# Edge tiles of 128 rows in two gather stages, and the edge network moved from the first of them into the second

## The chip, the cores and the metric

The kernel runs on one core of a Trainium2 chip. The metric is the device time of one execution in microseconds, the lower the better. The five engines of the core each run their own instruction stream in order: PE (TensorE, matrix products), DVE (VectorE), ACT (ScalarE), POOL (GpSimd) and SP (SyncE, which here only issues transfers). They meet through semaphores. Transfers run on the core's 16 DMA engines.

## The reference, cut to what matters

Two layers of a graph network on 6250 nodes (N) of 256 features (D) with 100000 edges (E), sorted by their destination. In both layers each node gets a sum over its incoming edges, of rows of the source nodes. In the second layer each row is weighted first, by four numbers of the edge; these are its attribute (4 values, `edge_attr_4`) times one number that a small network makes of the edge's 10 other values:

```
x -> layer norm -> xn
layer 0: agg[dst] += xn[src] for all edges;  MLP with batch norm of agg
         linear attention over all nodes;  mixture of experts        -> xm
layer 1: rad  = silu(edge_attr_10 @ fc_w1 / sqrt(10)) @ fc_w2 * 1.679177 / 8
         msg[dst] += (edge_attr_4 * rad) (x) xm[src] for all edges, then 7 maps of 64x64
         linear attention;  mixture of experts                        -> out
```

## The kernel before

The program is a chain of phases, each a block in which all engines work through a list of their own, with a barrier between blocks. Four of them matter here.

**p0** loads `src` and `dst`, turns them so that edge k*125+p stands in partition p, column k, of `idx` and `dstf`, normalises x into `xn_d`, works out tables for the later stages (`rel`, `left`, `left0`, `base`) and writes these to memory.

**g1** is the first gather stage. For each of 800 tiles of 125 edges (`NTILE`, `TN`) POOL issues an indirect transfer that fetches 125 rows of `xn_d` into `got` (`gather`, line 752), DVE makes a one-hot matrix of the destinations (`make_hot`, line 869), and PE multiplies the two into one or two sums for a block of 125 nodes (`sums`, line 1017). In the same block run: the projections of the linear attention (`QKV`, every 12 steps), its output (`ATT`, every 9 steps), the first layer of the MLP (`UPS`), and the edge network (`RAD`): 200 units of 500 edges, every 3.5 steps, each a transposition of the edge values (`turn_emb`, line 1097), a copy on ACT (`copy_emb`, line 814), a product (`hidden_of`, line 1101), a Silu on ACT (`do_silu`, line 819), and a multiplication and a sum on DVE (`reduce`, lines 957 and 960). At its end `scale_attr` multiplies the attributes, and `turn_weights` and `copy_weights` turn them into `wts`.

**The middle** (p5 and what follows) is the mixture of experts. It is not changed.

**g2** is the second gather stage: 400 groups of two tiles (`NG`). POOL issues two gathers for a group (line 2054), DVE makes the one-hot matrix (line 1803) and multiplies it by the four weights for each of the two tiles (`weighted`, line 1808), PE does four products (line 1818, `edge_sums`), and DVE adds the result to a ring of node sums (`accumulate`, line 2128). In the first half of the stage run the keys and values of the second attention (`KV`, a node tile every 4 steps: `project` line 2226, `square` line 2082, `size` line 2141, `roots` with a Sqrt on ACT line 2089, `scale_k` line 2154, `products` line 2236); in the second half the node tiles are finished (`P9`, from step 211 on, line 2267 and others, with a root on POOL, line 1194).

The order of the work on each engine is set by `timeline`, which is called with the same number of steps on all engines; a plan is a list of start steps and of functions with lags. A function with lag 4 of a unit that starts at step 10 is written into its engine's stream at step 14. Inside one step the order is that of the plans, and in a plan that of its list. How far POOL may run ahead is set by the slots of `got` (`GR` = 16 tiles in g1, `GB` = 10 groups in g2), how far DVE, by those of `hot` (`HR`), and `BANKS` holds the PSUM banks of g2 in which sums of groups may stand before DVE has added them. An fp32 product shows in the profile as two MATMUL instructions.

```
def timeline(n_steps, *plans):
    starts = [({s: i for i, s in enumerate(when)}, stages) for when, stages in plans]
    for s in range(n_steps):
        for at, stages in starts:
            for fn, lag in stages:
                if s - lag in at:
                    fn(at[s - lag])
```

## Time and profile before

| what | value |
|---|---|
| median of 3 runs | 3891.04 us (3885.07 to 3892.74) |
| profiled execution | 3889.95 us, span 3888.2 us |
| mean granted clock of TensorE | 0.92 |
| PE busy | 3174.3 us (82%) |
| POOL busy | 2399.7 us (62%) |
| DVE busy | 2088.2 us (54%) |
| ACT busy | 991.0 us (25%) |
| gathers of g1, first and last start | 88.7 and 1411.0 us |
| gathers of g2, first and last start | 2190.7 and 3445.8 us |

The two gather stages take two thirds of the time. "Busy" of an engine is an average over stages that have different limits; a stage is read by windows of its own.

### The profile page before, as it was taken

To read this page: it belongs to the slowest core of one execution; us is meant where nothing else is said; L and a number is where in the kernel's file an instruction comes from. 1 tells how busy PE (TensorE), PEld (TensorE's weight loads), DVE (VectorE), ACT (ScalarE), POOL (GpSimd) and SP (SyncE) were. 2 spreads that over 40 slices of the span, in tenths; PEclk is the share of its full clock that TensorE was granted. 3 is DMA by queue.
4 is the path that set the end of the run, shared out by engine and by line. 5 is a ranking of instruction groups with operands and counts; after the bars stand their busy time and mean duration, and the time that the engine had idled before them with its cause. 6 is when DMAs were issued, how large, how long until landed. Compare 5 with 4: busy or idle time off the path is not lost. (4 is left out here: it accounts for less than half of the span.)

```text
span 3888.2 us, 50625 instructions
## 1 busy us (share of the span) xinstructions
PE 3174.3 (82%) x14564; PEld 2517.1 (65%) x14564; DVE 2088.2 (54%) x5926; ACT 991.0 (25%) x2271; POOL 2399.7 (62%) x2116
## 2 busy tenths in 40 slices
PE   0699999999999969949992488888878778758998
PEld 0356667666777758838881366666677667747787
DVE  4354446666666635643336666666656555542333
ACT  2365552222222115513331211111101100002221
POOL 3688888888888742654341477788788888830000
PEclk9899999999999979969995699999999988879999
DMA  6544445555555544663327643333345544432222
GB/s 172 134 118 115 117 115 160 143 143 144 146 153 153 141 123 159 204 180 93 93 86 228 173 102 96 96 96 96 98 124 145 132 124 120 126 102 72 65 72 55
DMA packets 476922, 487.35 MB, mean 125 GB/s; under 512 B 247179, under 2 KB 413733, under 8 KB 476569
## 3 DMA queue, kind: packets, MB, share of 16 engines
q0 software_dynamic: 222784, 233.84, 23.9%
q1 hardware_dynamic: 243310, 237.70, 21.5%
q10 hardware_dynamic: 10575, 12.80, 1.0%
q8 instruction: 113, 1.85, 0.2%
q14 instruction: 140, 1.15, 0.1%
HBM read 361.48 MB, written 120.81 MB: 124 GB/s over the span
## 5 line engine op out<-in xcount | busy, mean ns | idle before, releaser
L752 POOL DMA_INDIRECT g_got<-xn_d,idx x800 | 1021.1, 1276 | 254.8 <-issue 193.4
L2054 POOL DMA_INDIRECT g_got<-xm_d,idx x800 | 987.4, 1234 | 251.4 <-issue 236.8
L1818 PE MATMUL ps<-g_hotw,g_got 125*128 125x192 f32 (+1 forms) x3200 | 590.6, 336 | 247.5 <-DMA g_got<-xm_d,idx 244.5
L1818 PEld LDWEIGHTS ps<-g_hotw,g_got 125*128 125x128 f32 x3200 | 538.4, 208 | 311.2 <-DMA g_got<-xm_d,idx 281.5
L1017 PE MATMUL ps<-g_got,g_hot 125*125 125x256 f32 x2506 | 677.8, 398 | 28.6 <-DMA g_got<-xn_d,idx 23.3
L1017 PEld LDWEIGHTS ps<-g_got,g_hot 125*125 125x125 f32 x2506 | 440.2, 191 | 209.6 <-issue 108.0
L1194 POOL TENSOR_TENSOR p_ln_rs<-p_ln_pre,neg_half 125x2 f32<-125x2 f32 x75 | 52.3, 697 | 622.4 <-DVE p_ln_pre L1189 622.4
L2128 DVE TENSOR_TENSOR g_ring<-g_ring,ps 128x336 f32 x400 | 201.9, 505 | 335.3 <-PE ps L1818 229.6
L1808 DVE TENSOR_TENSOR g_hotw<-g_hot,wts 125x192 f32<-125x192 f32 x800 | 253.0, 357 | 13.8
L869 DVE TENSOR_SCALAR g_hot<-iota,dstf 125x125 f32<-125x125 f32 (+1 forms) x800 | 251.4, 364 | 3.4 <-PE ps L1017 3.3
L1736 POOL DMA_INDIRECT z_d<-p_yj,p_to x108 | 122.3, 1132 | 200.9 <-DVE p_to L1759 179.1
L1377 PE MATMUL ps<-gin_w,p_hid 128*125 128x256 f32 x800 | 180.5, 385 | 23.2 <-ACT p_hid L1340 23.2
L2462 PE MATMUL ps<-p_w,p_hid 128*125 128x256 f32 x800 | 179.3, 382 | 23.1 <-ACT p_hid L2475 23.1
L2226 PE MATMUL ps<-g_wkv,g_kT 128*125 128x512 f32 x400 | 197.1, 638 | 0.0
L1136 PE MATMUL ps<-g_hT,g_w 128*128 128x250 f32 x800 | 192.1, 384 | 3.8 <-ACT g_hT L826 3.8
L2462 PEld LDWEIGHTS ps<-p_w,p_hid 128*125 128x125 f32 x800 | 148.0, 187 | 54.0 <-ACT p_hid L2475 31.5
L1377 PEld LDWEIGHTS ps<-gin_w,p_hid 128*125 128x125 f32 x800 | 150.3, 190 | 45.7 <-issue 23.5
L2451 PE MATMUL ps<-p_f3T,p_w 128*128 128x250 f32 x800 | 175.1, 375 | 4.6 <-DMA p_f3T<-f3T_d 4.6
L1136 PEld LDWEIGHTS ps<-g_hT,g_w 128*128 128x128 f32 x800 | 155.3, 196 | 24.4 <-ACT g_hT L826 4.6
L819 ACT ACTIVATE g_hs<-ps 100x320 f32<-100x320 f32 x200 | 87.2, 436 | 316.6 <-PE ps L1101 314.2
L2451 PEld LDWEIGHTS ps<-p_f3T,p_w 128*128 128x128 f32 x800 | 151.4, 189 | 25.0 <-DMA p_f3T<-f3T_d 5.3
L2267 PE MATMUL ps<-wm,g_ring 128*125 128x256 f32 x700 | 163.7, 386 | 0.0
(322 smaller groups left out, 4803.9 us busy)
## 6 DMA issues: line engine op xcount, KB each, us to landing
h_d<-g_hid SPq DMA_DIRECT2D x25, 1000.0 KB
p_hid<-h_d SPq DMA_DIRECT2D x25, 1000.0 KB
p_xr<-jobs_d SPq DMA_DIRECT2D x54, 258.0 KB
g_got<-xn_d,idx POOLq DMA_INDIRECT x800
g_got<-xm_d,idx POOLq DMA_INDIRECT x800
p_wj<-z_d SPq DMA_DIRECT2D x50, 224.0 KB
g_own<-xn_d SPq DMA_DIRECT2D x50, 125.0 KB
q_d<-g_qo SPq DMA_DIRECT2D x25, 250.0 KB, 3.5
```

What stands on the lines that cost most here:

```text
L752: landed.start(e.indirect_dma_start(got[:, k % GR, :], None, xn_d[0:N, :], bass.IndirectOffsetOnAxis(ap=idx[:, k:k + 1], axis=0)), k % GR)
L869: ready.done(e.tensor_scalar(hot[:, k % HR, 0:n], iota4[0:TN, 0:n], dstf[:, k:k + 1], -float(lo * TN), ALU.subtract, ALU.is_equal), "hot")
L1017: mm = e.matmul(ps[0:TN, b % 2, 0:D], hot[:, k % HR, (b - lo) * TN:(b - lo + 1) * TN], got[:, k % GR, :], start=(OPENS[b] == k), stop=(CLO ...
L1136: mm = e.matmul(ps[:, 5 + n % 3, k * BN:(k + 1) * BN], w1[:, c, f:f + P], hT[:, i % 2, c, :], start=(c == 0), stop=(c == DC - 1))
L1377: mm = e.matmul(ps[0:TN, u, t * D:(t + 1) * D], hid[:, u, c, t * TN:(t + 1) * TN], w2[:, c, :], start=(c == 0), stop=(c == HC - 1))
L1808: return [e.tensor_tensor(to[:, j, :, :], hot[:, j, :].unsqueeze(1).broadcast_to([TN, 4, WIN]), weights[:, j, :].unsqueeze(2).broadcast_to ...
L1818: mm = e.matmul(ps[:, bank, at:at + n], rows[j][:, c * P:(c + 1) * P], rhs, start=(j == 0), stop=(j == 1))
L2054: landed.start(e.indirect_dma_start(got[:, 2 * (g % GB) + j, :], None, xm_d, bass.IndirectOffsetOnAxis(ap=idx[:, 2 * g + j:2 * g + j + 1], ...
L2128: added.done(e.tensor_tensor(to, to, ps[:, BANKS[g % 4], 0:SL * WIN].rearrange("p (k n) -> p k n", k=SL), ALU.add), "add")
L2226: mm = e.matmul(ps[0:TN, bank, :], kT[:, i % 2, c, :], wkv[:, c, at:at + INNER], start=(c == 0), stop=(c == DC - 1))
L2451: mm = e.matmul(ps[:, q, m * BN:(m + 1) * BN], w1[:, k, c, f * P:(f + 1) * P], f3T[:, u, :, c * TN:(c + 1) * TN], start=(c == 0), stop=(c ...
L2462: mm = e.matmul(ps[0:TN, 4 + u, t * D:(t + 1) * D], hid[:, u, k, f, t * TN:(t + 1) * TN], w2[:, k, f, :], start=(j == 0), stop=(j == 2 * F ...
```

## The change

- A tile has 128 edges instead of 125. 782 tiles (391 groups) take the place of 800 (400); the last tile has 96 empty places, whose destination is -1. All tiles and tables of edges have 128 partitions. `src` and `dst` are loaded as 96 rows of 1024 and two single rows, and `edge_attr_4` as one transfer of 97 rows of 1024 edges and one of the rest. The turned attributes go to `wts` in g1 as before, but without the factor `rad`.
- The edge network leaves g1. In g2 it runs as 196 units (`NU`) of four tiles, one every second step: `turn_emb` at lag 2, `copy_emb` at 3, `hidden_of` and `do_silu` at 4, `radial` on DVE at 5. The groups start at step 6 (`FIRST`). `radial` makes `wr`, the weights times `rad`, which `weighted` and `weigh` use.
- In g2 the weighting of the second tile of a group is done by ACT (`weigh`, four activations of 48 columns, whose scale is a value per partition); DVE keeps that of the first. PE waits for both.
- Slots: `GR` 16 to 20, `HR` of g1 10 to 12, `LEAD` of g1 7 to 8, `GB` 10 to 12; `BANKS` of g2 four to three, the fourth holds the edge network.
- The code for stray edges (p3f, p8f) is changed alike. It does not run: worked out from the inputs, no edge lies outside its window, in tiles of 125 as of 128.

```diff
-GE = 2 * TN
-NG = E // GE
-RR = 100
-RU = E // RR
-ST = RU // TN
+NTILE = -(-E // P)
+NG = NTILE // 2
+PADS = NTILE * P - E
+ST = 8
+RU = ST * P
+RR = -(-E // RU)
...
# g1
-            GR, HR, SR, RG, LEAD, AR = 16, 10, 4, 12, 7, 3
-            got = ph.sb("got", [TN, GR, D])
+            GR, HR, SR, RG, LEAD, AR = 20, 12, 4, 12, 8, 3
+            got = ph.sb("got", [P, GR, D])
...
-            RAD = [10 + 7 * i // 2 for i in range(NU)]
-            WTS = every(RAD[-1] + 12, 4, ST)
+            WTS = every(90, 20, ST)
...
-                        e.dma_start(attr[:, :, :], A["edge_attr_4"].rearrange("(r u) k -> r u k", r=RR)).then_inc(s_attr, 16)
+                        e.dma_start(attr[0:RR - 1, :, :], A["edge_attr_4"][0:(RR - 1) * RU, :].rearrange("(r u) k -> r u k", u=RU))\
+                         .then_inc(s_attr, 16)
...
-                             (RAD, [(do_silu, 5), (copy_emb, 3)]))
...
-                             (RAD, [(reduce, 7)]), (WTS[0:1], [(scale_attr, 0)]), (WTS, [(copy_weights, 3)]))
+                             (WTS, [(copy_weights, 3)]))
...
-                             (RAD, [(hidden_of, 5), (turn_emb, 3)]), (WTS, [(turn_weights, 3)]))
+                             (WTS, [(turn_weights, 2)]))
...
# g2
-            GB, HR, BANKS, LEAD, P9R = 10, 7, (0, 1, 2, 7), 3, 4
+            GB, HR, BANKS, LEAD, P9R, FIRST, RL = 12, 7, (0, 1, 2), 3, 4, 6, 6
...
-            GROUPS = range(NG)
-            KV = every(2, 4, NT)
+            GROUPS = every(FIRST, 1, NG)
+            RAD = every(0, 2, NU)
+            KV = every(FIRST + 2, 4, NT)
...
+                    def weigh(g):
+                        u = g % HR
+                        ready.wait(e, g, "hot")
+                        rads.wait(e, g // 2, "wr")
+                        summed.wait(e, g - HR, "sums")
+                        for k in range(4):
+                            ins = e.activation(hotw[:, u, 1, k, :], hot[:, u, 1, :], ACT.Copy,
+                                               scale=wr[:, (g // 2) % RL, 2 * (g % 2) + 1, k:k + 1])
+                        ready1.done(ins, "hotw")
...
-                    timeline(LAST_STEP, (ZERO, [(zero, 0)]), (KV, [(square, 3), (roots, 5)]), (P9, [(copy, 10)]))
+                    timeline(LAST_STEP, (GROUPS, [(weigh, 1)]), (RAD, [(do_silu, 4), (copy_emb, 3)]), (ZERO, [(zero, 0)]), (KV, [(square, 3), (roots, 5)]), (P9, [(copy, 10)]))
...
+                    def radial(i):
...
+                        silu.wait(e, i, "silu")
+                        rads.done(e.tensor_tensor(hwr[:, u, :, :], hs[:, u, :, :],
+                                                  w2r[:, :].unsqueeze(1).broadcast_to([P, UU, C1]), ALU.mult), "mul")
+                        rads.wait(e, i, "mul")
+                        rads.done(e.tensor_reduce(rad[:, u, :], hwr[:, u, :, :], AX, ALU.add), "sum")
...
+                        rads.done(e.tensor_tensor(wr[:, i % RL, :, :], wts[:, UU * i:UU * (i + 1), :],
+                                                  rad[:, u, :].unsqueeze(2).broadcast_to([P, UU, 4]), ALU.mult), "wr")
...
-                             (GROUPS, [(make_hot, 1)]),
-                             ([0], [(centre, 1)]), (KV, [(accumulate_kv, 8), (scale_k, 6), (size, 4)]),
+                             (RAD, [(radial, 5)]), (GROUPS, [(make_hot, 1)]), ([FIRST], [(centre, 1)]),
+                             (KV, [(accumulate_kv, 8), (scale_k, 6), (size, 4)]),
...
                         ready.wait(e, g, "hotw")
+                        ready1.wait(e, g, "hotw")
                         added.wait(e, g - len(BANKS), "add")
...
+                    def turn_emb(i):
...
+                        silu.wait(e, i - 1, "silu")
+                        eturn.done(e.transpose(ps[0:UU * K1, 7, UU * C1:UU * C1 + P],
+                                               emb[:, i % 4, :, :].rearrange("p j f -> p (j f)"), ident[:, :]), "turn")
...
-                    timeline(LAST_STEP, (GROUPS, [(sums, LEAD)]), (KV, [(products, 7), (project, 2)]),
+                    timeline(LAST_STEP, (GROUPS, [(sums, LEAD)]), (RAD, [(hidden_of, 4), (turn_emb, 2)]), (KV, [(products, 7), (project, 2)]),
```

On ACT, in the first half of g2, one node tile's work stood in the stream so before (`g_sq` and `g_v` are the squares and the copy of keys and values, `g_rs` the Sqrt):

```order
L2082 ACTIVATE g_sq<-ps 125x512 x2
L2084 ACTIVATE g_v<-ps 125x512
L2089 ACTIVATE g_rs<-g_pr 125x8
L2082 ACTIVATE g_sq<-ps 125x512 x2
L2084 ACTIVATE g_v<-ps 125x512
```

and the same four steps stand so now (`g_hotw` is `weigh`, `g_hs` the Silu, `g_embT` the copy of the edge values):

```order
L2146 ACTIVATE g_hotw<-g_hot,g_wr 128x48 x4
L2153 ACTIVATE g_embT<-ps 40x128
L2132 ACT_TABLE_LOAD
L2132 ACTIVATE g_rs<-g_pr 125x8
L2146 ACTIVATE g_hotw<-g_hot,g_wr 128x48 x4
L2158 ACT_TABLE_LOAD
L2158 ACTIVATE g_hs<-ps 128x256
L2146 ACTIVATE g_hotw<-g_hot,g_wr 128x48 x4
L2153 ACTIVATE g_embT<-ps 40x128
L2125 ACTIVATE g_sq<-ps 125x512 x2
L2127 ACTIVATE g_v<-ps 125x512
```

Sixteen small activations, two copies, two Silu and two loads of a function table per node tile have come in; a load stands ahead of each Sqrt and ahead of the Silu that follows it.

On PE, at the same place, the stream before was (`g_hotw,g_got` are the sums of a group, `g_wkv` the projection, `g_k,g_v` the products):

```order
L2226 MATMUL ps<-g_wkv,g_kT 125x512 x4
L1818 MATMUL ps<-g_hotw,g_got 128x192 x2
L1818 MATMUL ps<-g_hotw,g_got 128x144 x2
L2236 MATMUL ps<-g_k,g_v 128x128 x4
L1818 MATMUL ps<-g_hotw,g_got 128x192 x2
L1818 MATMUL ps<-g_hotw,g_got 128x144 x2
```

and is now:

```order
L2325 MATMUL ps<-g_wkv,g_kT 125x512
L1771 MATMUL ps<-g_hotw,g_got 128x192
L1771 MATMUL ps<-g_hotw,g_got 128x144 x2
L2335 MATMUL ps<-g_k,g_v 128x128 x3
L1771 MATMUL ps<-g_hotw,g_got 128x192
L1771 MATMUL ps<-g_hotw,g_got 128x144 x2
L2312 MATMUL ps<-g_w1b,g_embT 128x256
L2307 MATMUL ps<-ident,g_emb 40x128
```

Behind every second group stand the product of one unit of the edge network (`hidden_of`, line 2312) and, directly behind it, the transposition of the next (`turn_emb`, line 2307), which waits for the Silu of the first.

On SP, in g1 at step 40, one transfer changes its shape. Before:

```order
L729 DMA g_attr<-in_edge_attr 100x4000
L730 DMA g_w<-in_L_gnn_W 128x2x1024
```

Now:

```order
L721 DMA g_attr<-in_edge_attr 97x4096
L723 DMA g_attr<-in_edge_attr 1x2688
L725 DMA g_w<-in_L_gnn_W 128x2x1024
L726 DMA gin_w<-in_L_gnn_W 128x8x256
L728 DMA g_vecs<-in_L_gnn_b 128x8x1
```

It stands ahead of all later loads of g1, in one queue with them.

## Rows read from the trace of the kernel before

**Rows 1.** Indirect transfers on POOL by line: ns min/median/max, first and last start.

```profile
L752 POOL DMA_INDIRECT g_got<-xn_d,idx x800: 1207/1212/2794, 88.7 to 1411.0; - x160
...
L2054 POOL DMA_INDIRECT g_got<-xm_d,idx x800: 1207/1211/1976, 2190.7 to 3445.8; - x160
...
L1736 POOL DMA_INDIRECT z_d<-p_yj,p_to x108: 956/961/1701, 1753.0 to 2050.6; - x108
...
L1442 POOL DMA_INDIRECT jobs_d<-p_rows,p_slots x100: 1184/1188/1416, 1533.1 to 1727.1; - x100
```

**Rows 2.** Timeline of g2, one gather: start, us; in brackets POOL's idle time.

```profile
2211.47 1.21 POOL L2054 DMA_INDIRECT g_got<-xm_d,idx  x1 [0.30 <-issue]
```

**Rows 3.** Windows: PE, PEld, DVE, ACT, POOL busy (instructions), granted clock, DMA share, GB/s.

```profile
76.00:86.00 10.00, 0.00 (x0) 0.00 (x0) 0.00 (x0) 0.00 (x0) 0.00 (x0) 1.00 0.28 77
165.00:170.00 5.00, 0.00 (x0) 0.00 (x0) 0.00 (x0) 0.00 (x0) 3.81 (x4) 0.50 1.03 217
400.00:600.00 200.00, 192.59 (x774) 125.27 (x772) 90.68 (x252) 105.28 (x200) 161.62 (x127) 0.99 0.46 115
800.00:1000.00 200.00, 185.12 (x808) 136.74 (x807) 129.26 (x332) 47.19 (x130) 164.43 (x135) 0.97 0.53 143
2400.00:2600.00 200.00, 165.55 (x795) 125.29 (x793) 132.39 (x358) 31.38 (x67) 160.10 (x132) 0.93 0.39 96
3000.00:3200.00 200.00, 159.21 (x793) 141.94 (x792) 110.35 (x339) 22.36 (x79) 163.33 (x140) 0.90 0.50 129
```

**Rows 4.** Groups of POOL instructions by shape, whole span: the roots of g2.

```profile
L1194 POOL TENSOR_TENSOR g_ln_rs<-g_ln_pre,neg_half 125x1 f32<-125x1 f32 x50 | 30.1, 602 | 17.9 <-DVE g_ln_pre L1189 16.6
```

**Rows 5.** Groups of PE instructions by shape, 85 to 1500 us.

```profile
L1101 PE MATMUL ps<-g_w1b,g_embT 50*100 50x320 f32 x400 | 156.7, 472 | 1.4 <-ACT g_embT L814 1.3
...
L1097 PE MATMUL ps<-ident,g_emb 100*50 100x100 f32 x200 | 50.9, 255 | 61.6 <-DMA g_emb<-in_edge_attr 40.4 <-ACT g_hs L819 21.0
```

**Rows 6.** Timeline of g1, issues on SP: start, us, what.

```profile
154.00 0.51 SPq L729 DMA_DIRECT2D g_attr<-in_edge_attr  x1
...
181.53 1.28 SPq L718 DMA_DIRECT2D g_emb<-in_edge_attr  x3
```

**Rows 7.** Timeline of g2, PE around one node tile.

```profile
2217.35 3.60 PE L2226 MATMUL ps<-g_wkv,g_kT 128*125 128x512 f32 x8
...
2220.79 1.30 PE L1818 MATMUL ps<-g_hotw,g_got 125*128 125x192 f32 x8
...
2221.93 1.08 PE L2236 MATMUL ps<-g_k,g_v 125*128 125x128 f32 x8
```

**Rows 8.** Timeline of g1, one unit of the edge network.

```profile
499.66 0.78 PE L1101 MATMUL ps<-g_w1b,g_embT 50*100 50x320 f32 x2
...
500.47 0.44 ACT L819 ACTIVATE g_hs<-ps 100x320 f32<-100x320 f32 x1 [0.93 <-PE ps L1101]
...
501.06 0.25 PE L1097 MATMUL ps<-ident,g_emb 100*50 100x100 f32 x1
```

**Rows 9.** Groups of ACT instructions by shape, 85 to 1500 us.

```profile
L819 ACT ACTIVATE g_hs<-ps 100x320 f32<-100x320 f32 x200 | 87.2, 436 | 316.6 <-PE ps L1101 314.2
L819 ACT ACT_TABLE_LOAD x45 | 57.7, 1283 | 0.8
L814 ACT ACTIVATE g_embT<-ps 50x100 f32<-50x100 f32 x200 | 49.2, 246 | 241.1 <-PE ps L1097 241.0
...
L1340 ACT ACTIVATE p_hid<-p_hid,gin_bias,gin_scale 128x250 f32<-128x250 f32 x50 | 25.1, 583 | 38.2 <-DMA p_hid<-h_d 38.2
```

**Rows 10.** The same of ACT, 2185 to 3500 us.

```profile
L2089 ACT ACTIVATE g_rs<-g_pr 125x8 f32<-125x8 f32 x50 | 10.4, 209 | 184.4 <-DVE g_pr L2145 184.4
L2089 ACT ACT_TABLE_LOAD x1 | 1.3, 1283 | 0.0
```

**Rows 11.** Groups of DVE instructions by shape, 2185 to 3500 us.

```profile
L2128 DVE TENSOR_TENSOR g_ring<-g_ring,ps 128x336 f32 x400 | 201.9, 505 | 335.3 <-PE ps L1818 229.6 <-issue 100.7
L1803 DVE TENSOR_TENSOR g_hot<-iota,g_rel 125x96 f32<-125x96 f32 x400 | 101.6, 254 | 5.5 <-DMA g_base<-base_d 5.5
...
L2191 DVE TENSOR_TENSOR g_x<-ps,g_xb 125x256 f32<-125x256 f32 x50 | 21.2, 424 | 70.1 <-PE ps L2267 70.1
```

More of the change, by code:

```diff
@@ L62 @@
 RING1 = RB * TN
+RADIAL = 1.679177 / 8.0
 class Steps:
@@ L307, in gps_kernel @@
             normed = ph.steps("normed", "t0", "t1")
+            full = 96
             with nc.Block() as block:
@@ L1866, in _ @@
                             e.sem_inc(s_dve, 1)
+                            e.sem_inc(s_act, 1)
+                @block.scalar
+                def _(e):
+                    some = e.value_load(flag0[0:1, 1:2], min_val=0, max_val=E)
+                    with e.If(some > 0):
+                        with e.Fori(0, NG) as g:
+                            e.wait_ge(s_eT, 1)
+                            e.activation(embT[:, :], ps[0:2 * K1, 2, 0:P], ACT.Copy).then_inc(s_ec, 1)
+                            e.wait_ge(s_hid, 1)
+                            e.activation(hs, ps[:, 3, 0:2 * C1].rearrange("p (j c) -> p j c", j=2), ACT.Silu,
+                                         scale=K1 ** -0.5).then_inc(s_silu, 1)
+                            e.wait_ge(s_act, 1)
+                            e.sem_clear(s_act)
                 @block.tensor
```

369 lines of the change are left out of this document (213 added, 156 removed).

## The prediction

> **What bounds the kernel now.** I read the gathers first. In each gather stage POOL issues 800; one takes 1.21 us [rows 1], and 0.30 us of issue time stands ahead of it [rows 2], so the shortest interval is 1.51 us. 800 of them are 1208 us. g2 lasts 1255 us from its first gather to its last [rows 1]; with 50 roots of 0.60 us and their 0.30 [rows 4], 45 us, the 1253 us are full. POOL's issue rate is the bound of all of g2. In g1 the same sum is about 1255 us of 1322. Then the windows [rows 3]: PE is busy 193 of 200 us in g1 at 400 us, 185 at 800, and 166 and 159 of 200 in g2. So PE stands close behind POOL in g1, and has some 17 to 20% of air in g2, at a granted clock of 0.93 and 0.90, which is between the two levels of 1.2 and 2.4 GHz. DVE and ACT have air everywhere.
>
> **Tiles of 128 rows.** 18 gathers fewer per stage would be 27 us each. But the rows say more: the scatter of the middle stage that takes 128 rows costs 0.96 us, its neighbour with 125 rows 1.19 us, like the gathers with 1.21 [rows 1]. I take 0.985 us for a gather of 128 rows, 1.285 us with the issue time; bounds: 0.96 and 1.21. POOL then needs 782 x 1.285 = 1005 us a stage plus roots, and PE or a chain of waits becomes the bound in both.
>
> **g1 without the edge network.** Between 400 and 600 us PE works 192.59 us for 127 gathers, 1.52 us each [rows 3]. The edge network is (156.7 + 50.9) / 200 = 1.04 us per unit [rows 5], one in 3.5 steps, 0.30 us per gather; groups overlap by some 10%, so 0.27. It leaves 1.25 us for PE and 1.285 for POOL; the two don't mesh perfectly, I take 1.34 us for the first 313 tiles: 419 us. Between 800 and 1000 us it is 185.12 us for 121 gathers (135 instructions less some 14 roots), 1.53, less four fifths of 0.27, 1.31; POOL has 1.285 plus a root in nine steps, 1.39. I take 1.43 us for the other 469: 671 us. The start of the block: in the last ten microseconds of p0 no engine works, while transfers run at a share of 0.28 of the 16 engines [rows 3]; those are the tables, of 125 rows each. With 128 rows I expect them to spread wider, and 5 us less. Ten microseconds pass before PE has its first rows.
>
> **The transfer of 97 rows.** 0.28 of 16 engines is 4.5 [rows 3]; five is the largest number up to 16 that divides 125. If a transfer's rows are dealt out by such a divisor, the 97 rows of 16 KB of the attributes, a prime number, go through one engine. 77 GB/s on 4.5 engines is 17 GB/s each, 217 GB/s at full share 13.5 [rows 3], so 1589 KB take 93 to 117 us. All later loads of SP's queue stand behind it, `load_xn` of step 50 first, which PE needs at step 55. That gives PE 15 steps of work, 21 us, then it stands still for 72 to 96 us; I take 85. Before, SP needed from 154.0 to 181.5 us [rows 6] for the same place, and that lies in the 1411. The bounds are thus 30 and 96 us. The Trainium skill ("DMA: Bandwidth & Descriptors", section "Why a DMA increments its semaphore by 16 and not by 1") states this rule, the largest k up to 16 that divides the slowest dimension; the share of 0.28 agrees with it, and no row here shows a prime.
>
> So the last gather of g1 starts at 84 + 10 + 419 + 671 + 85 = 1269 us in place of 1411: -142 us.
>
> **g2, first half.** What POOL gives, the edge network takes here. Per node tile (four steps, four groups) PE has 4 x 1.30 + 3.60 + 1.08 = 9.9 us [rows 7], and before waits for POOL's 8 x 1.51 = 12.1 us. Now two units come in, and in PE's stream the transposition of the next unit stands directly behind the product of this one and waits for its Silu. Product to Silu's start is 0.81 us for 320 columns [rows 8], 0.7 for 256; the Silu is 0.38 (0.436 and 0.246 us for 320 and 100 columns give 0.86 ns a column) [rows 9]. During this PE does nothing, and what ACT has ahead of the Silu counts. An activation of 48 columns is 0.24 us by that line; its scale per partition adds some 0.1 (0.583 us for 250 columns with two such operands, against 0.375) [rows 9]; as they overlap I take 0.26, 1.05 for the four of `weigh` (bounds 0.8 and 1.4). The order now has two table loads per node tile, ahead of the Sqrt and of the Silu behind it, where g2 had one in all [rows 10]; one is 1.28 us [rows 9].
>
> From the Silu of an even step without load to that of the next even step the chain is: DVE finishes its heavy step and adds a group (0.50 us and its issue gap of 0.25 [rows 11]), 1.0; `radial`, two operations of 256 columns at 0.42 [rows 11] and a small one, 1.1; one-hot 0.25 and signals 0.1; on ACT four weightings 1.05, copy 0.27, load 1.28, Sqrt 0.21 [rows 10], four weightings 1.05, load 1.28, Silu 0.38. Together 8.0 us, of which PE could use 3.4. The other half is PE's: transposition 0.3, projection 3.6, sums 1.3, products 1.1, sums 1.3, product to Silu's end 1.1, together 8.7, at a clock like that of 2400 us [rows 3] 9.2. So 17.2 us per tile against 12.1, over 50 tiles +255 us. Six steps of prelude: +5.
>
> **g2, second half.** No Sqrt, no loads. Before, a group takes 2 x 1.51 + 0.26 x 0.9 = 3.27 us, PE works 159.21/200 of it [rows 3], 2.60 us, 2.5 at a better clock. Added per group: half a unit, (0.25 + 0.5)/2, and half of the wait of 0.7 us behind its product: 3.2 us. POOL has 2.8. 180 groups at 3.2 are 576 us against 192 at 3.27, 628: -52. DVE gives up one weighting per group for `radial`, and the ring of three banks costs nothing while PE waits for ACT. Sum of g2: +208 us.
>
> **Sum.** Profiled execution 3889.95 (the median is 3891.04): 3890 - 142 + 208 = 3956 us, 1.7% slower.
>
> **The rivals.**
> - *ACT's chain is hidden* (faster). Then g2's first half is PE-bound: 9.9 + 2 x 0.75 + 2 x 0.7 = 12.8 us, 13.0 with clock, +45; g2 -2, total 3746. For it: ACT's work is some 10 us per tile. Against it: the order is fixed, and loads stand between two products that PE waits on. It decides if the Silu behind a load starts under 1 us after its product. 0.18.
> - *The 97 rows go through many engines*: 54 us less, 3902. 0.17.
> - *A gather of 128 rows still costs 1.21 us*: g1 stays with POOL, 782 x 1.51 + 49 + what isn't covered of the stall, -30; g2's second half +13; total 4081. For it: the row of 0.96 is a scatter, no gather. 0.08.
> - *A switch of tables costs more than its load.* If PE's wait grew by as much again as the load, 100 x 1.28 us, it were 4084. Against it: 45 loads among ACT's work had 0.8 us of idle time ahead of them in all [rows 9]. 0.04. The Trainium skill ("ScalarE: Activation LUTs", section "What ACT_TABLE_LOAD costs") names a drain of 1.38 us beside the load of 1.28; by it the sum would be 4094 us, and no row here shows the drain.
> - The forecast has the rest, 0.53.
>
> **Numbers.** The unknown prices give the forecast 3870 to 4060 of its own (weightings 0.8 to 1.4 us, 50 to 100 us over the tiles; meshing in g1, 40). The range 3790 to 4100 leaves out most of the first rival and the ends. Faster by over 0.2%: the first rival, 0.18, a part of the second and the low end of the forecast, 0.10: 0.28. Within 0.2%, about what a measurement of this kernel can tell from none: 0.05. Slower 0.67.
>
> **What would show it.** Gathers of 0.96 to 1.0 us on POOL in both stages. In g1 one wait of PE of 70 to 100 us near step 55, at about 180 us, and steps of 1.34 us after. In g2 PE's longest total wait is the edge transposition for ACT's Silu, 50 times some 4 us and 150 times under 1; node tiles every 17 us in the first half, groups of 3.2 us in the second; about 100 table loads. The prediction is wrong above all if gathers don't get shorter, if the long stall isn't there, or if the first half of g2 takes under 13.5 us per tile.

## The result, and the profile after

The changed kernel takes 4349.24 us in the median of its runs (4336.68, 4342.79, 4355.68 and one stray execution in the slow state of 15807.3 us, which the ratio leaves out); the kernel before takes 3891.89 us beside it. The ratio is 1.1165, 95% interval 1.1127 to 1.1204: 11.7% slower, where 1.7% was forecast. The profiled execution took 4336.68 us, its span 4335.1. The direction was right and the size was not.

The gathers of the changed kernel, by line: ns min/median/max, first and last start. They answer to [rows 1].

```profile
L748 POOL DMA_INDIRECT g_got<-xn_d,idx x782: 943/949/2187, 81.3 to 1413.4; - x196
L2097 POOL DMA_INDIRECT g_got<-xm_d,idx x782: 943/949/2845, 2196.5 to 3887.0; - x196
```

A gather costs POOL 0.949 us in place of 1.21, as forecast. Yet g1 lasts 1332 us from first to last start (before 1322), g2 1690 us (before 1255). For the halves of g2, the projections of K and V in both kernels, which end with the first half (the kernel before, then the changed one):

```profile
L2226 PE MATMUL ps<-g_wkv,g_kT x400: 590/592/1061, 2208.7 to 2802.4; 128*125 128x512 f32 x134
```

```profile
L2325 PE MATMUL ps<-g_wkv,g_kT x400: 592/1057/1187, 2232.6 to 3130.5; 128*125 128x512 f32 x134
```

The profiled executions differ from the forecast stage by stage:

| stretch | before | forecast | after | off by |
|---|---|---|---|---|
| start to g1's last gather | 1411.0 | 1269 | 1413.4 | +144 |
| to g2's first gather | 779.7 | 779.7 | 783.1 | +3 |
| g2 to the last projection | 611.7 | 872 | 934.0 | +62 |
| to g2's last gather | 643.4 | 591 | 756.5 | +165 |
| rest | 442.4 | 442.4 | 448.1 | +6 |

The sum is 380 us, which is 4336.7 - 3956. 309 us of it lie in g1 and in the second half of g2, outside the stretch for whose chain of ACT the forecast has its largest term. Windows of the changed kernel (columns as in [rows 3]):

```profile
400.00:600.00 200.00, 171.73 (x706) 128.09 (x705) 63.14 (x200) 40.56 (x105) 131.70 (x135) 0.93 0.43 120
800.00:1000.00 200.00, 154.47 (x686) 130.57 (x687) 99.33 (x266) 27.44 (x64) 120.26 (x130) 0.90 0.45 135
2400.00:2600.00 200.00, 143.70 (x595) 94.88 (x594) 99.64 (x264) 104.33 (x287) 84.88 (x88) 0.85 0.27 68
3200.00:3400.00 200.00, 164.06 (x801) 136.90 (x800) 106.14 (x327) 85.33 (x334) 106.86 (x117) 0.92 0.48 122
```

In g1 neither PE (154 of 200 us at 800 us, before 185) nor POOL (120) is full, and the granted clock is lower than before. Something stands between them.

**PE's results come late.** The timeline at one of those places, PE and then DVE:

```profile
795.36 0.60 PE L1047 MATMUL ps<-g_qt,g_ksd 128*128 128x125 f32 x4
795.80 3.19 PE L983 MATMUL ps<-g_got,g_hot 128*125 128x256 f32 x14
807.54 2.07 PE L1054 MATMUL ps<-g_mix,g_qz 128*125 128x256 f32 x4 [8.56 <-DVE g_qz L911]
```

```profile
793.60 0.34 DVE L848 TENSOR_SCALAR g_hot<-iota,dstf 128x250 f32<-128x250 f32 x1
804.87 0.42 DVE L907 TENSOR_SCALAR g_den<-ps 128x250 f32<-128x250 f32 x1 [10.92 <-remote]
```

PE's records show the denominators done at 795.96 us. DVE, which waits for just them and has nothing else to do, starts at 804.87, and PE then waits 8.56 us for DVE's quotient. Such a wait of DVE is named "remote" or "issue" here, since the profile finds no work that ends just before it. The trace also holds the times at which PE's semaphores count up, and they show that it is the signals that are late. Up to 789.5 us each comes 0.014 us after the end that is recorded for its matmul. That of the denominators comes at 804.84. The last five of the stretch, for work whose recorded ends lie between 797.69 and 810.47 us, come together between 811.17 and 811.38, and a wait of DVE for one of them ends with it, at 811.27. They stand for more than ten matmuls, which the records have 0.2 us apart at best, and these can't be done in 0.2 us: the work was done earlier and the signals were held. Counted over the trace, 14 of g1's 50 divisions start more than 1 us after PE's recorded end with DVE idle (13 of them over 3 us, the longest 11.3); in the kernel before none does. It happens behind dense runs of sums. The clock falls behind it: window of the last idle stretch.

```profile
800.00:805.00 5.00, 0.00 (x0) 0.00 (x0) 0.13 (x1) 0.00 (x0) 3.78 (x5) 0.94 0.40 118
805.00:808.00 3.00, 0.46 (x1) 0.46 (x2) 2.93 (x5) 0.00 (x0) 2.09 (x4) 0.50 0.33 100
```

Once PE is back, its clock is at the lower of its two levels, 0.50 (1.2 GHz). No term of the prediction had this.

**The stall of the attributes** is there. SP's queue, the window behind it, and PE's wait in it:

```profile
158.52 21.63 SPq L723 DMA_DIRECT2D g_attr<-in_edge_attr  x1
180.19 2.12 SPq L725 DMA_DIRECT2D g_w<-in_L_gnn_W  x1
182.35 9.60 SPq L726 DMA_DIRECT2D gin_w<-in_L_gnn_W  x1
191.99 34.77 SPq L728 DMA_DIRECT2D g_vecs<-in_L_gnn_b  x1
...
233.51 1.05 SPq L98 DMA_DIRECT2D g_xn<-xn_d  x2
```

```profile
195.00:225.00 30.00, 0.00 (x0) 0.00 (x0) 0.00 (x0) 0.00 (x0) 0.00 (x0) 0.50 0.11 40
```

```profile
PE ps L993 <- DVE g_xr L862: 64.9, 1, 64.9
```

SP sits 75 us on the issues behind the transfer of 97 rows, while the transfers use 0.11 of the 16 engines; PE has no rows of x for 64.9 us (85 forecast). In the trace's list of DMA packets the 97 of 16 KB stand one behind the other, from 159.4 to 227.4 us, most of them 0.61 us long: this is one engine's work, at 27 GB/s where the forecast took 13.5 to 17.

**The chain of ACT in g2.** One node tile, PE and ACT:

```profile
2415.90 5.12 PE L2325 MATMUL ps<-g_wkv,g_kT 128*125 128x512 f32 x8
...
2424.12 0.70 PE L2312 MATMUL ps<-g_w1b,g_embT 40*128 40x256 f32 x2
2425.39 0.27 PE L2307 MATMUL ps<-ident,g_emb 128*40 128x128 f32 x1 [0.56 <-ACT g_hs L2158]
...
2429.49 0.70 PE L2312 MATMUL ps<-g_w1b,g_embT 40*128 40x256 f32 x2 [1.35 <-issue]
2433.71 0.37 PE L2307 MATMUL ps<-ident,g_emb 128*40 128x128 f32 x1 [3.52 <-ACT g_hs L2158]
2433.87 3.70 PE L2325 MATMUL ps<-g_wkv,g_kT 128*125 128x512 f32 x4
```

```profile
2428.27 1.01 ACT L2146 ACTIVATE g_hotw<-g_hot,g_wr 128x48 f32<-128x48 f32 x4 [3.03 <-DVE g_hwr L2193]
2429.19 0.25 ACT L2153 ACTIVATE g_embT<-ps 40x128 f32<-40x128 f32 x1
2429.46 1.28 ACT L2132 ACT_TABLE_LOAD   x1
2430.75 0.21 ACT L2132 ACTIVATE g_rs<-g_pr 125x8 f32<-125x8 f32 x1
2430.87 1.00 ACT L2146 ACTIVATE g_hotw<-g_hot,g_wr 128x48 f32<-128x48 f32 x4
2431.88 1.28 ACT L2158 ACT_TABLE_LOAD   x1
2433.18 0.38 ACT L2158 ACTIVATE g_hs<-ps 128x256 f32<-128x256 f32 x1
```

From projection to projection 17.97 us (17.2 forecast), with the waits in the order forecast: PE 3.52 us for the Silu behind two loads, ACT 3.03 us for DVE. The weightings, 1.01 us for four, are those of the forecast (1.05). PE's projection takes 5.12 us where [rows 7] has 3.60: its granted clock stood at 0.50 from 2415.46 to 2418.87 us, after the wait. What ACT waits for is DVE's one-hot, and DVE has `radial` ahead of it. Behind the other Silu of the tile, DVE starts `radial` 0.04 us after the Silu's end:

```profile
2415.62 0.43 DVE L2193 TENSOR_TENSOR g_hwr<-g_hs,g_w2r 128x256 f32<-128x256 f32 x1 [1.04 <-ACT g_hs L2158]
2416.63 0.25 DVE L1757 TENSOR_TENSOR g_hot<-iota,g_rel 128x96 f32<-128x96 f32 x1
2416.91 1.01 ACT L2146 ACTIVATE g_hotw<-g_hot,g_wr 128x48 f32<-128x48 f32 x4 [1.33 <-DVE g_hot L1757]
```

Before the 3.03 us it isn't the Silu that DVE waits for, which ended at 2425.24: it is still at the tile's sizes and at a ring addition, and starts `radial` at 2426.92 and the one-hot at 2427.92.

### The profile page after: what moved, and what is told of

Read it like the earlier page. It is cut to its first block and busy times, and to the rows that moved or that the text cites. A ratio compares the mean times of both kernels' runs of the same rounds, so it can differ in the third digit from the quotient of the medians.

```text
span 4335.1 us, 52668 instructions
## 1 busy us (share of the span) xinstructions
PE 3234.6 (75%) x14424; PEld 2570.4 (59%) x14424; DVE 1955.1 (45%) x5665; ACT 1368.9 (32%) x3838; POOL 1913.6 (44%) x2084
## 5 line engine op out<-in xcount | busy, mean ns | idle before, releaser
L2097 POOL DMA_INDIRECT g_got<-xm_d,idx x782 | 760.7, 973 | 642.9 <-PE ps L1771 378.2
L748 POOL DMA_INDIRECT g_got<-xn_d,idx x782 | 759.9, 972 | 407.0 <-issue 199.0
L983 PE MATMUL ps<-g_got,g_hot 128*125 128x256 f32 x2450 | 629.8, 399 | 23.5 <-issue 12.0
L2146 ACT ACTIVATE g_hotw<-g_hot,g_wr 128x48 f32<-128x48 f32 x1564 | 394.3, 323 | 557.7 <-DVE g_hot L1757 324.0
L983 PEld LDWEIGHTS ps<-g_got,g_hot 128*125 128x125 f32 x2450 | 477.9, 200 | 128.3 <-issue 46.5
L1771 PE MATMUL ps<-g_hotw,g_got 128*128 128x192 f32 (+1 forms) x3128 | 534.1, 322 | 1.4 <-ACT g_hotw L2146 0.8
L1771 PEld LDWEIGHTS ps<-g_hotw,g_got 128*128 128x128 f32 x3128 | 499.2, 200 | 47.1 <-issue 30.9
L848 DVE TENSOR_SCALAR g_hot<-iota,dstf 128x250 f32<-128x250 f32 (+1 forms) x782 | 226.1, 338 | 13.7 <-remote 7.9
L2325 PEld LDWEIGHTS ps<-g_wkv,g_kT 128*125 128x125 f32 x400 | 111.1, 293 | 135.3 <-issue 134.4
L2312 PE MATMUL ps<-g_w1b,g_embT 40*128 40x256 f32 x392 | 138.7, 434 | 65.3 <-ACT g_embT L2153 44.3
```

What stands on the lines that cost most here:

```text
L748: landed.start(e.indirect_dma_start(got[:, k % GR, :], None, xn_d[0:N, :], bass.IndirectOffsetOnAxis(ap=idx[:, k:k + 1], axis=0)), k % GR)
L848: ready.done(e.tensor_scalar(hot[:, k % HR, 0:n], iota4[:, 0:n], dstf[:, k:k + 1], -float(lo * TN), ALU.subtract, ALU.is_equal), "hot")
L983: mm = e.matmul(ps[0:TN, b % 2, 0:D], hot[:, k % HR, (b - lo) * TN:(b - lo + 1) * TN], got[:, k % GR, :], start=(OPENS[b] == k), stop=(CLO ...
L1771: mm = e.matmul(ps[:, bank, at:at + n], rows[j][:, c * P:(c + 1) * P], rhs, start=(j == 0), stop=(j == 1))
L2097: landed.start(e.indirect_dma_start(got[:, 2 * (g % GB) + j, :], None, xm_d, bass.IndirectOffsetOnAxis(ap=idx[:, 2 * g + j:2 * g + j + 1], ...
L2146: ins = e.activation(hotw[:, u, 1, k, :], hot[:, u, 1, :], ACT.Copy, scale=wr[:, (g // 2) % RL, 2 * (g % 2) + 1, k:k + 1])
```

## The experiments

Kernels of one group ran on one chip. The table has, from each profile, the stretches of the table above; a node tile is the mean distance of the projections of the 50 tiles, a group the second half by its gathers. "Late" counts g1's divisions that start over 3 us late, as above.

| run | total, us (median) | g1 | g2 first half | g2 second half | us per node tile | us per group | late |
|---|---|---|---|---|---|---|---|
| before | 3892 | 1322 | 612 | 643 | 12.1 | 3.2 | 0 |
| after | 4349 | 1332 | 934 | 756 | 18.2 | 4.2 | 13 |
| e1 | 4402 | 1353 | 935 | 791 | 18.2 | 4.4 | 12 |
| e2 | 4176 | 1276 | 931 | 660 | 18.2 | 3.7 | 0 |
| e3 | 4345 | 1298 | 935 | 794 | 18.2 | 4.4 | 14 |
| e4 | 4092 | 1357 | 716 | 703 | 13.9 | 3.9 | 15 |
| e5 control | 4395 | 1361 | 935 | 787 | 18.2 | 4.4 | 13 |
| e6 | 4268 | 1300 | 933 | 729 | 18.3 | 4.0 | 6 |
| e7 | 4366 | 1342 | 937 | 779 | 18.3 | 4.3 | 15 |
| e8 | 4018 | 1428 | 632 | 634 | 12.5 | 3.5 | 3 |
| e9 | 3960 | 1071 | 919 | 649 | 18.2 | 3.6 | 0 |
| e10 | 4245 | 1340 | 927 | 669 | 18.2 | 3.7 | 0 |
| e11 | 3756 | 1089 | 705 | 646 | 13.7 | 3.4 | 0 |
| e12 | 3589 | 1088 | 629 | 565 | 12.2 | 3.1 | 0 |
| e13 control | 4399 | 1358 | 931 | 786 | 18.3 | 4.3 | 13 |
| e14 | 4216 | 1360 | 843 | 737 | 16.4 | 4.1 | 12 |
| e15 | 4087 | 1303 | 761 | 706 | 14.9 | 3.7 | 12 |
| e16 control | 4410 | 1365 | 936 | 798 | 18.2 | 4.4 | 14 |
| e17 | 4430 | 1372 | 935 | 810 | 18.2 | 4.5 | 17 |
| e18 | 3852 | 1223 | 710 | 615 | 13.8 | 3.2 | 0 |

Groups, with the number of the chip on record: e1 to e4 (0), e5 to e8 (3), e9 to e12 (11), e13 to e15 (0), e16 and e17 (1), e18 alone (4), without a control. e1, e2, e7, e10 and e18 leave edges out of the sums, e9 and e17 fetch a part of each row; they show where time goes and are no candidates. The kernel before took 3888 to 3894 us in the median of each group.

### First group: rows, engines, the attributes, the order

**e1**, the sums over 125 of 128 rows; **e2**, the gathers too:

```diff
-landed.start(e.indirect_dma_start(got[:, k % GR, :], ..., ap=idx[:, k:k + 1]
+landed.start(e.indirect_dma_start(got[0:TN, k % GR, :], ..., ap=idx[0:TN, k:k + 1]
-mm = e.matmul(ps[0:TN, b % 2, 0:D], hot[:, ...], got[:, k % GR, :]
+mm = e.matmul(ps[0:TN, b % 2, 0:D], hot[0:TN, ...], got[0:TN, k % GR, :]
```

(and the same in g2; e1 has the last two lines alone).

> The changed kernel, but the matmuls of the gathered rows in g1 and g2 contract 125 of the 128 rows; the gathers still fetch 128. (Leaves the last 3 edges of each tile out of the sums.) In the changed kernel's trace, results of PE reach their consumers 5 to 11 us later than its recorded work ends, 14 times ahead of the divisions of g1 alone, always behind a dense run of sums, and never before the change. Theory C, the 128-row contraction slows or holds PE: those waits vanish, g1 and the second half of g2 get 150 to 250 us shorter together, total 4100 to 4200 us. Theories A (PE is simply held up when it works through a backlog densely) and B (transfers spread over all engines hold PE up): nothing changes, 4349 within 15 us.

> As the run before it, and the gathers fetch 125 rows as before the change, so that they cost 1.21 us on POOL again and land later. (Leaves the last 3 edges of each tile out.) Theory B, the 128-row transfers hold PE up: the late results vanish, g2's second half falls from 4.2 to about 3.3 us per group (-160 us), g1 becomes POOL-bound at 1.51 us per gather plus the stall, its last gather starts at about 1350 to 1400 us; total 4150 to 4220. Theory A, a dense PE: POOL's 1.51 us per gather keeps PE from running dense, so late results become rarer too, but the groups of g2's second half, where PE has 80% of the time, stay at 3.8 us or more; total 4270 to 4400. Gathers of 1.21 us are what both expect; if they take 0.95, neither has understood POOL's cost.

e1 took 4402 us, the control of the next group, on another chip, 4395, and the results are late as before (12 of them): what PE contracts plays no part. e2 took 4176, with gathers of 1.214 us, and not one late result. The waits of DVE for the denominators in g1, e2 and then the control e5 (total us, times, longest):

```profile
DVE g_den L907 <- PE ps L1047: 24.4, 9, 5.6
DVE g_den L907 <- issue: 4.5, 2, 4.1
```

```profile
DVE g_den L907 <- remote: 132.3, 15, 13.8
DVE g_den L907 <- issue: 29.8, 6, 8.3
DVE g_den L907 <- PE ps L1047: 20.8, 8, 6.1
```

So the gathers of 128 rows are what makes the kernel slower here, by 226 us against e1 on the same chip: they hold up PE's results. A dense PE alone does not: the kernel before, with 125 rows, has PE busy for 192.59 of 200 us [rows 3] and not one late result. e2 changes two things at once, the form of the transfer and, with 1.214 us on POOL, the pace.

**e3**, the attributes in two transfers:

```diff
-e.dma_start(attr[0:RR - 1, :, :], ...)
+for lo, hi in ((0, 96), (96, RR - 1)):
+    e.dma_start(attr[lo:hi, :, :], ...)
```

> The changed kernel with the 97 attribute rows loaded as 96 and 1. My theory (one transfer of 97 rows goes through one engine, and SP's later loads stand behind it): the stall of PE at 180 us, 65 us in the trace of the changed kernel, falls under 15 us; g1's last gather starts 55 to 85 us earlier, total 4265 to 4295. Rival (the stall is something else at the start, such as the eight weight transfers or the vectors with single-element runs in front of it): under 15 us of change.

Behind the split, SP's window shows all engines at work:

```profile
158.00:176.00 18.00, 8.41 (x31) 6.69 (x29) 2.64 (x7) 2.94 (x8) 11.04 (x12) 0.81 1.02 278
```

1.02 of the engines and 278 GB/s against 0.11 and 40: the theory of one engine holds. PE's longest wait for those rows is 8.4 us (64.9 before). g1 is 55 to 60 us shorter than in e1 and e4, which have its code otherwise, and the total of 4345 is 56 under e1's. The theory's 55 to 85 us are there; the total expected, 4265 to 4295, was missed, since it started from the first measurement of the changed kernel (4349), which was 46 to 60 us under all three controls.

**e4**, the transposition one step later: `(RAD, [(hidden_of, 4), (turn_emb, 3)])` in place of `(turn_emb, 2)` in PE's order.

> The changed kernel with the transposition of the edge values one step later in PE's order of g2, so that the sums of a step stand between the product of one unit and the transposition of the next, and PE does not wait for the Silu with nothing to do. Theory of the prediction (PE and ACT hand the chain to and fro): the wait of the transposition for Silu shrinks from 3.5 us to 2 in the steps with a table load and to nothing in the others, node tiles of the first half fall from 18.0 to 15.5 to 16.5 us, total -75 to -150 us. Rival (ACT's own work and the table loads are the chain, PE only waits along): node tiles stay at 17.5 to 18, total within 25 us.

The expected 75 to 150 us were over 300 against e1 and the controls: 219 us in g2's first half and 88 in the second. A node tile takes 13.9 us in place of 18.2. PE's wait for the Silu is gone; between 2300 and 2900 us what is left is mostly the wait for the copy of the transposed values:

```profile
PE ps L2312 <- ACT g_embT L2153: 56.5, 34, 2.1
```

My count of the chain was right for the order as written, but not how much of it one step of slack takes away: I take it that the links between PE, ACT and DVE had been closed in a ring, and that this opens it.

### Second group: is it density or spread, and the tiles alone

> The changed kernel, nothing edited, on the same chip as the three runs beside it: its g1 took 1332 us from first to last gather in its first profile, in other kernels with the same code of g1 1353 and 1357. I expect 4330 to 4400 us in total, and g1 and g2 within 40 us of 1345 and 1715.

e5, nothing edited, took 4395 us.

**e6** fills 128 x 128 elements on POOL ahead of each gather.

> The changed kernel with a fill of 128 x 128 elements on POOL ahead of every gather (0.21 us and its wait), so that gathers of 128 rows are issued about every 1.5 us, as gathers of 125 rows are. Theory A (PE is held up because it works through a backlog densely): like the run with 125-row gathers, late results of PE vanish, g1 1276 us, g2's second half 3.5 us per group, total within 40 us of 4176. Theory B (transfers of 128 rows, spread over all 16 engines, hold PE up): late results stay, ahead of g1's divisions more than 8 of over 4 us; POOL's slower issue comes on top, total 4340 to 4480.

The interval of the gathers became 1.34 us, not 1.5: the fill of 0.22 us replaced part of the issue time.

```profile
701.10 0.95 POOL L754 DMA_INDIRECT g_got<-xn_d,idx  x1 [0.17 <-POOL g_idle L752]
702.04 0.23 POOL L752 MEMSET g_idle<- 128x128 f32 x1
702.44 0.95 POOL L754 DMA_INDIRECT g_got<-xn_d,idx  x1 [0.17 <-POOL g_idle L752]
```

4268 us, 127 under the control, with 6 late results for 13 and the longest 4.4 us. Slowing POOL down makes the kernel faster. It is between the theories: the pace counts, and since the interval stayed under e2's 1.51 us, the run does not tell what 128 rows would do at that pace.

**e7** gathers and sums 126 rows.

> The changed kernel with gathers and sums of 126 rows (leaves the last 2 edges of each tile out). 14 divides 126. If the share of engines is the largest divisor of the row count up to 16, POOL's cost is near that of 128 rows, 0.94 to 0.97 us, and the late results are there as in the control, total within 40 us of it. If 128 is special (a power of two, all partitions), the gather takes 1.2 us and the total comes out near the 4176 of 125 rows.

1.001 us per gather, late results as in the control. So nothing is special about 128. The Trainium skill ("DMA: Bandwidth & Descriptors", section "Why a DMA increments its semaphore by 16 and not by 1") has the largest k up to 16 that divides the slowest dimension, which is 16 for 128 rows, 14 for 126, 5 for 125 and 4 for 124. The traces agree with it by the packets of a gather. They are of 4096 bytes, four rows, with the rest of each engine's share behind them: 125 rows show 5 such rests of one row, 126 show 14, 124 show 4 of three rows, and 128 rows go in 32 whole packets, or, with 64 columns (e9), in 16 of 2048 bytes, one to a share. With the small packets beside them a gather of 128 rows is 48 packets, of 126 rows 64, of 125 rows 128, of 124 rows 144, and POOL's cost follows: 0.949 us, 1.001, 1.214 and 1.292 (e10). The gathers that make results late are thus those with the fewest packets.

**e8**, the tiles of 128 rows alone: the edge network back in g1, in units of four edges a row, the weighting on DVE.

```diff
+RAD = [10 + 11 * i // 4 for i in range(NU)]
...
-GB, HR, BANKS, LEAD, P9R, FIRST, RL = 12, 7, (0, 1, 2), 3, 4, 6, 6
+GB, HR, BANKS, LEAD, P9R, FIRST = 12, 7, (0, 1, 2, 7), 3, 4, 0
```

> Tiles of 128 rows alone: the edge network stays in g1 (units of four edges a row, 256 of them), the weighting stays on DVE, the rings of g1 are those of before. By the prediction's terms: POOL 782 x 1.285 = 1005 us and 45 of roots in g2, PE 2.6 us per group, so g2 1050 to 1090 us against 1255; g1 PE-bound at 1.55 us per tile, 1230 to 1300 us with the stall taken away; total 3890 - 180 - 50 = 3660 us, 3600 to 3720. If transfers of 128 rows hold PE up wherever PE has little air (theory B), g1 takes 1350 to 1450 us and g2 1150 or more; total 3830 to 3950.

4018 us, 3.2% slower than before (1.0304 to 1.0345), though POOL's gathers are cheaper by a fifth. g2, where nothing but the tile height and two more slots of `got` differ from before, takes 1266 us against 1255: the gain of 165 to 205 us that POOL's time promised is not there, and 31 results of g2's sums come over 3 us late in the trace. g1 is 106 us longer than before, with 3 late divisions; I didn't take its waits apart, and its edge network also has other units and loads than before.

### Third group: bytes, four engines, and ACT's part

**e9** fetches 64 of the 256 columns of each row, **e10** gathers and sums 124 rows.

> The changed kernel with gathers of 128 rows that fetch 256 bytes a row in place of 1024 (sums run at full width over rows of which three quarters are zeros; the output is not the sum wanted). Same number of transfers, rows and engines, a quarter of the bytes. If what holds PE's results up is the bytes (engines and SBUF writes busy), late results ahead of g1's divisions, 13 of over 3 us in the control, fall to 3 or fewer and the total comes to 4180 to 4250 us. If it is the number of pieces or their completions, spread over 16 engines, they stay at 10 or more and the total within 40 us of the control's 4395.

> The changed kernel with gathers and sums of 124 rows (leaves the last 4 edges of each tile out). The largest divisor of 124 up to 16 is 4: if engines follow divisors, this goes over 4 engines, costs POOL 1.2 to 1.3 us and shows no late results, total within 30 us of the 4176 of 125 rows. If only the distance to 128 counts, it is like 126 rows, 1.0 us and 4366.

**e11** moves the root: `kroot.done(e.tensor_tensor(rs, pr, neg_half, ALU.pow))` on POOL for ACT's Sqrt and DVE's reciprocal. **e12** moves the weighting:

```diff
-timeline(LAST_STEP, (GROUPS, [(weigh, 1)]), (RAD, [(do_silu, 4), (copy_emb, 3)]), ...
+timeline(LAST_STEP, (RAD, [(do_silu, 4), (copy_emb, 3)]), ...
+ready1.done(weighted(e, hotw[:, u, :, :, :], hot[:, u, :, :], wr[...], 1), "hotw")
```

> The changed kernel with the inverse root of the K sizes in g2 on POOL as a power of -0.5, as the other roots are, in place of Sqrt on ACT and a reciprocal on DVE: no table load is left between the Silus. The prediction's chain has two loads of 1.28 us per node tile on it: node tiles of the first half fall from 17.7 to 14.8 to 15.7 us, g2 from 1722 to 1570 to 1620. Rival (loads lie beside PE's own waits): under 40 us. Rival of a drain beside the load: up to twice the fall, g2 1500 or less.

> The changed kernel with both halves of the weighting on DVE, as before the change. The prediction's chain has 2 x 1.05 us of ACT's weighting per node tile on it and gives DVE 0.36 us more twice: node tiles 17.7 to 16.0 to 16.6 us, g2 60 to 90 us shorter; total 4310 to 4340. Rival (DVE's part of the chain grows by as much, or ACT's part is hidden): within 25 us of the control. In the second half the same way of counting gives nothing to 20 us.

All four came out beside what was expected. g1, whose code e11 and e12 don't touch, takes 1088 us instead of 1361, without one late result. DVE's waits for the denominators in e12, and the gathers:

```profile
DVE g_den L907 <- PE ps L1047: 57.0, 23, 6.9
```

```profile
L748 POOL DMA_INDIRECT g_got<-xn_d,idx x782: 942/947/1407, 81.7 to 1170.1; - x196
```

So e9 told nothing of bytes. e10, which has no late results either, took 4245 us with gathers of 1.292 us, 69 more than e2 with 1.214. In g2 the node tiles of the unedited order take 18.2 us with late results and without (e9 and e10 as every control), so the edits can be read: without loads 13.7 us, 4.5 less where I had 2 to 3 (the edit takes out DVE's reciprocal too); without the weighting 12.2 us, 6.0 less where I had 1.1 to 1.7. e11's g2 of 1351 us would fit the rival of a drain (1500 or less), but 141 us of it are the second half without late results, and in e12 both loads are still there: the timeline of e12, ACT and PE.

```profile
2424.75 0.27 ACT L2153 ACTIVATE g_embT<-ps 40x128 f32<-40x128 f32 x1 [0.45 <-PE ps L2308]
2425.04 1.28 ACT L2132 ACT_TABLE_LOAD   x1
2426.33 0.21 ACT L2132 ACTIVATE g_rs<-g_pr 125x8 f32<-125x8 f32 x1
2426.56 1.28 ACT L2158 ACT_TABLE_LOAD   x1
2427.86 0.39 ACT L2158 ACTIVATE g_hs<-ps 128x256 f32<-128x256 f32 x1
```

```profile
2427.12 0.70 PE L2313 MATMUL ps<-g_w1b,g_embT 40*128 40x256 f32 x2
2428.39 0.27 PE L2308 MATMUL ps<-ident,g_emb 128*40 128x128 f32 x1 [0.57 <-ACT g_hs L2158]
```

ACT copies as soon as PE has turned, loads, roots, loads, and is ready 0.04 us after the product; PE waits 0.57 us. With the weighting in its queue ACT stood still for 3.03 us ahead of weighting and copy: the weighting waits for DVE's one-hot, which stands behind `radial` and, in this unit, behind the tile's sizes; `radial` in turn needs ACT's last Silu. The price of `weigh` on this chip was this queueing behind DVE, not its 1.01 us. Where results come late the edit gives less: e14 has 16.4 us against 18.3 of its control.

### Fourth to sixth group: chip or edit

> The changed kernel unedited, beside the run of the weighting on DVE. Two edits of g2 alone brought g1, whose code they don't touch, from 1361 to 1088 us in the job before this one, and no result of PE came late there. Theory X (it is a property of the chip or of where things lie in a job, not of the edit): sometimes the control too has g1 at 1080 to 1100 us and a total of 3900 to 3960. Theory Y (the edit of g2 makes g1 fast, through the placement of code or tiles): g1 stays at 1330 to 1365 us, total 4340 to 4400, beside fast edits on the same chip.

> The kernel with the weighting on DVE again, so that it and the control are on one chip. Theory Y: 3589 us again, g1 1088. Theory X: it goes with the control of this job: g1 1340 to 1360 if the control has that, and then some 3830 to 3870 us in total.

> The changed kernel with four edits: weighting on DVE, inverse root on POOL, transposition one step later, attributes in 96 and 1 rows. g2's first half is then bounded by PE, 9.9 + 1.5 us per node tile and waits, 12.0 to 12.8 us, g2 1110 to 1170 us. With g1 at 1035 to 1060 (the stall of 50 us gone) total 3470 to 3540 us; if g1 takes 1300 in this job, 3720 to 3800.

Theory X holds: the kernel that took 3589 us took 4216 here (4180.95 to 4254.33, the profiled execution is the longest), where 3830 to 3870 were expected, with the late results back; e13, unedited, 4399. The same window of g1 in e12 and in e14:

```profile
700.00:900.00 200.00, 190.31 (x896) 163.32 (x895) 127.92 (x340) 34.53 (x81) 156.28 (x167) 0.97 0.60 180
```

```profile
700.00:900.00 200.00, 156.74 (x684) 128.88 (x685) 103.88 (x278) 24.98 (x61) 122.13 (x132) 0.91 0.46 137
```

e15, all four edits, took 4087 where 3720 to 3800 were expected, no better than e4 with one: its node tiles take 14.9 us, where e11 and e4 have 13.7 and 13.9. POOL stands at the root for DVE (`POOL g_rs L2112 <- DVE g_pr L2231` 95.8 us between 2300 and 2900 us), ahead of the gathers in its queue; whether that is the reason was not tested.

> The changed kernel unedited, on whatever chip this job gets. On chips like that of the first, second and fourth job: 4390 to 4405 us, g1 1360. On one like that of the third job (g1 1088 in two kernels with the same g1, no late results of PE): g1 1075 to 1095, g2 1540 to 1600, total 3900 to 3980, which would be the forecast's 3956 by way of a g1 60 us shorter and a g2 some 100 us longer than forecast.

> The gathers of 128 rows with a quarter of the bytes again, beside a control. It took 3960 us with a g1 of 1071 us on the third job's chip, where other kernels had no late results either, so it told nothing. If the control beside it has late results and a g1 of 1360: bytes are the cause if g1 falls under 1150, the number of pieces and their completions over 16 engines if it stays over 1320; between them, both.

e16 took 4410 us, e17 4430 with 17 late results: a quarter of the bytes changes nothing. Nor is it the number of packets, since 125 rows have 128 of them and no late results, 128 rows 48, and e17's gathers 32. What is left is the number of engines that a gather goes through, and its pace; these two are not told apart.

> The kernel with the four edits (weighting on DVE, root on POOL, transposition a step later, attributes in two transfers), 4087 us where results of PE come late, with gathers and sums of 125 rows (leaves the last 3 edges of each tile out). If the spread over 16 engines is what holds PE's results up and the four edits have taken ACT's chain away, nothing but POOL's 1.51 us per gather bounds both stages: g1 1210 to 1260 us, g2 782 x 1.51 + 100 roots x 0.9 = 1270 and some start, 1260 to 1310 us, total 3790 to 3870 us, on any chip. Rival (the network in g2 or the three banks cost something of their own beside the chain): g2 1350 or more, total over 3900.

**e18** took 3852 us, 0.991 of before (0.9886 to 0.9935), within the 3790 to 3870 expected; g2 took 1325 us, a little over the 1260 to 1310. It sums 125 of 128 edges a tile, so it is no candidate. With transfers of 125 rows and the order opened, a group takes 3.2 us, as before the change. The first half of g2 has 13.8 us per node tile against 12.1, and g1 is 99 us shorter. That e18 has no late results says little: no kernel with 128 rows ran beside it. Its trace is like the third group's in one more thing. There, as in e18, the signals of g1's sums are all but complete in the record (780 to 782 of 782), while all other runs of the changed kernel and its edits, e2 among them, lack 15 to 27% of them (e2 has 632 of 782, the first measurement 637).

Of the kernels that compute everything, e11 and e12 beat the one before on the third group's chip, e12 by 7.8% (ratio 0.9223, 0.9197 to 0.925); on the fourth group's e12 is 8.2% slower. So no version that computes everything is found that is faster on every chip tried. Every execution here was recorded by the profiler, and since records of signals are missing in each run in which results come late, it is open whether the recording has a part in it; e2, which lacks as many signals and has no late result, shows that missing records alone don't make results late.

## Why the prediction was wrong in size

- **Tiles of 128 rows.** "I take 0.985 us for a gather of 128 rows": 0.949 measured. Right, and so was the divisor.
- **g1.** "It leaves 1.25 us for PE and 1.285 for POOL; the two don't mesh perfectly, I take 1.34 us" and 1.43 for the rest. This is the step that failed: it takes it that PE's results are there when its work ends. In the first measurement and in the first, second, fourth and fifth group they came up to 13 us late behind dense runs (e14), and what brings it on these chips is the gathers of 126 and 128 rows: 12 to 17 late divisions with them at full pace (3 in e8, whose g1 is another), none with 125 on the chip where 128 had 12. It cost 273 us of g1 (1361 against 1088, the same code on two chips; 244 against the first profile) and, by the same comparison, 107 to 138 us of g2's second half (756 and 787 against e9's 649). Where nothing is late, the term errs to the other side: g1's last gather starts at 1170 in e12, 1269 was forecast.
- **The transfer of 97 rows.** The mechanism was right, 85 us were forecast, 64.9 stand in the trace and 55 to 60 come out of e3. The transfer took 68 us where 93 to 117 stood, but PE ran out of work 14 us after it began and not 21, and other loads stood behind it, so the two errors partly cancel.
- **g2, first half.** The mechanism was right in place, order and about in size: 17.2 us against 18.2, 62 us in all with a start that was longer by some 10 us; the projections run at a lower clock, 1.057 us in the median for 0.592. The rival that ACT's chain is hidden did not come; with the weighting elsewhere it does, and e12 shows what that is worth on its chip, some 290 us of the first half (629 against 919 and 927 of e9 and e10). On the chip of e13 and e14 it is 88 us.
- **g2, second half.** "3.2 us" per group: 3.6 in e9 without late results, 4.2 to 4.4 with them. The term was too small even so: 58 us (649 against 591). I didn't settle which of ACT's waits makes it; e12, without the weighting, has 3.1.
- **The table loads.** No row shows a drain: the load at 2431.88 starts as the weighting ends (2430.87 + 1.00), and the Sqrt 0.01 us behind its load. A costlier switch is out as far as these rows go; e11 gains 4.5 us a tile where its two loads are 2.56, and what the rest is was not taken apart (its reciprocal went too, and the waits of three engines changed). The Trainium skill ("ScalarE: Activation LUTs", section "What ACT_TABLE_LOAD costs") names a drain of 1.38 us; the measurement decides, and here there is none to be seen.

Taken together, the 380 us are 351 of late results (244 and 107), 62 and 58 of g2's two halves, 9 of the other stages, and -99 of a g1 that is otherwise quicker than forecast. The split rests on a comparison of chips, since the unedited kernel never ran on the third group's. The nearest to it there is e9, the changed kernel with a quarter of the bytes, and it took 3960 us where the forecast is 3956. That is luck as much as skill: in e9 g1's last gather starts 112 us before the forecast, and the two halves of g2 are 47 and 58 us longer than forecast.

## What to carry to other kernels

Before work is put on an idle engine, walk the ring: what does each piece wait for, and does that stand behind a piece that waits for this engine? Sets of four activations, 1.01 us each, cost 6 us a tile on one chip and 2 on another, and one step of slack for the transposition took over 4 us back. When a transfer gets cheaper to issue, look at whether its consumers' signals still come on time: an idle engine whose wait ends at nothing recorded is a sign. And measure a kernel whose time depends on that on several chips, with the unedited kernel in every group.
